# Graph kernel on one core: chunk offsets kept in bytes, both PSUM addresses of a chunk lowered together, one load of offsets moved from chunk 60 to chunk 47

## The chip, the cores and the metric

The kernel runs on one core of a Trainium2 chip. The metric is the device time of one execution in microseconds (us). PE is TensorE's matmul side, PEld its weight load, DVE VectorE, ACT ScalarE, POOL GpSimd, SP SyncE. "PEldq" in the rows is TensorE's sequencer: the part that reads the instruction stream, executes register instructions itself and passes weight loads and matmuls on to the array's queue.

## The reference, cut to what matters

Inputs are `x` (1024 nodes x 512 features, fp32), 16384 edges `src`, `dst` (sorted by `dst`) with weights, and six weight matrices of 512x512 with their biases.

```python
A[src, dst] += edge_weight;  A = dinv * A * dinv          # dinv from the row sums of A
h = x
for l in 0, 1:
    h = leaky_relu(((A @ h) @ W_gcn[l] + b_gcn[l]) @ W_mlp[l] + b_mlp[l])
x = layernorm(x + h)
h = gcn_conv(relu(gcn_conv(x, W1, b1)), W2, b2)           # edge counts plus self loops, both sides scaled by deg^-1/2
out = layernorm(x + h)
```

## The kernel before, in words

**The chunk loop** builds the dense adjacency. The 16384 edges are cut into 128 chunks of 128 edges. For a chunk DVE makes a one-hot matrix of the sources (`sel`) and four matrices over a window of 12 destinations (`hot`: plain counts and the edge weight in three bf16 parts). PE then runs four matmuls with `sel` as the stationary operand, each adding into 8 strips of 12 columns in PSUM: the count into one bank, the three weight parts into another (`chunk(c)`, L696 to L703). Where in the bank the window begins depends on the data: it is `offsets[c]`, a register value. `window(c, kind)` (L672) turns it into an address, with `kind` 0 for the weights and 1 for the counts, one bank of 512 fp32 further on.

**The offsets.** DVE computes them at the head of the kernel, in elements, and copies them from PSUM to the row `off_row` as int32 (L976). `load_offsets(c0)` (L666 to L670) loads 16 of them into 16 of the 32 registers and makes a value of each (`snap`). The eight calls stand in PE's stream: one ahead of the loop, and after chunks 15, 31, 47, 60, 73, 86 and 105 (the table `loads`, L248; L784). The registers are two halves of 16 that are used in turn, so the load for chunks 64 to 79 may stand anywhere after chunk 47. After chunk 60 there is also a `value_load` of a flag (L788), which says whether the data fit the windows.

**Work between the chunks.** The destinations form 20 overlapping regions, each accumulated in a pair of banks. At `opening[r]` PE clears the pair (`clear`, L676, after ACT has evacuated region r-2); after `closing[r]` ACT copies it to SBUF, and DVE adds the overlapping ends. The table `fillers` (L236) puts fp32 work into PE's stream after named chunks: transposes of the weights, products of pairs of weight matrices (`split_product`, L648), biases (L748, L741). After chunk 47 stand 14 matmuls of 512 columns (6 at L648, 8 at L748), then the load for 48 to 63; after chunk 60 stand 8 transposes (L634), then the load for 64 to 79, then the flag. From chunk 35 on each chunk has a fifth matmul, for the degrees (L707).

**The other engines in the loop.** DVE's order is written by hand (L1085 to L1131): it makes the batches of `hot` and `sel` (L989 to L997), and between them the low halves of the weights (L1069, L1082). For batches 4 to 7 ACT makes a share of the last term of `hot` (L503), at named chunks. Semaphores `made`, `scaled`, `batch_used`, `region_done` and `evacuated` tie the three engines.

**After the loop** PE runs some 1,150 fp32 matmuls, transposes among them: A transposed times x, products with the weights, the layer norms' rows, the second graph network, to the end at 336.0 us.

Of the kernel before, what the change touches and what calls it, by code (L numbers as in the profile page):

```python
# [5 lines left out]
F32 = mybir.dt.float32  # L6
F32R = mybir.dt.float32r
BF16 = mybir.dt.bfloat16
I32 = mybir.dt.int32
ALU = mybir.AluOpType  # L10
ACT = mybir.ActivationFunctionType
AX = mybir.AxisListType

P = 128
BANK = 512
# [7 lines left out]
REGION = 52  # L23
# [7 lines left out]
def gnn_resnorm(nc, x, src, dst, weight, wg, bg, wm, bm, w1, b1, w2, b2, out):  # L31
# [35 lines left out]
    with ExitStack() as ctx:  # L67
# [108 lines left out]
        off_row = at("off_row", SM, [1, P], I32)  # L176
# [49 lines left out]
        max_row = small[0:1, 199:200]  # L226

        psum = ctx.enter_context(nc.psum_tensor("psum", [P, 8, BANK], F32))
        flat = psum.rearrange("p b n -> p (b n)")


        FILL, WIDE = (5, 6, 7), (4, 5, 6, 7)
# [12 lines left out]
        filling = [(name, i) for c in sorted(fillers) for name, i, k0, k1 in fillers[c] if k1 == KD]  # L245


        loads = {15: 16, 31: 32, 47: 48, 60: 64, 73: 80, 86: 96, 105: 112}  # L248
        ring += [("prep", 0, 5), ("prep", 1, 6), ("prep", 2, 7), ("prep", 3, 4), ("deg", 0, 4)]
        n_fill = [0]  # L250

# [20 lines left out]
        def bank(name, i=0):  # L272
            return psum[:, place[(name, i)], :]
# [31 lines left out]
        prep = sem("prep")  # L305
# [4 lines left out]
        off_ready, spill_ready, flag_ready = sem("off_ready"), sem("spill_ready"), sem("flag_ready")  # L310
# [300 lines left out]
        def _(pe):  # L611
# [52 lines left out]
            offsets = {}  # L664

            def load_offsets(c0):  # L666
                own = regs[c0 % (2 * G):c0 % (2 * G) + G]
                pe.load(own, off_row[0:1, c0:c0 + G])
                for j, r in enumerate(own):
                    offsets[c0 + j] = pe.snap(r, min_val=0, max_val=2 * BANK + REGION - 1)  # L670

            def window(c, kind):  # L672
                return flat[:, bass.ds(offsets[c] + kind * BANK, BANK)]\
                    .rearrange("p (h d) -> p h d", d=PITCH)[:, :, 0:WINDOW]

            def clear(r):  # L676
# [19 lines left out]
            def chunk(c):  # L696
                buf, own = where(c)
                stationary = sel[buf][:, own, :]
                for k in range(4):
                    moving = hot[buf][:, k, own, :].rearrange("p (h d) -> p h d", d=WINDOW)  # L700
                    ins = pe.matmul(window(c, 1 if k == 0 else 0), stationary, moving,  # L701
                                    start=False, stop=False, skip_group_check=True)
                return ins  # L703

# [54 lines left out]
            for c in range(CH):  # L759
                if c in batch_of:  # L760
                    pe.wait_ge(made, sets_made(batch_of[c]))
                    if batch_of[c] in SHARED:
                        pe.wait_ge(scaled, G * (1 + list(SHARED).index(batch_of[c])))
                for r in range(NR):
                    if opening[r] == c:
                        clear(r)
                ins = chunk(c)
                if c in closing:
                    ins.then_inc(region_done, 1)
                if c >= LATE_HW:  # L770
                    ins = degree(c)
                    if c + 1 in batch_of:
                        ins.then_inc(batch_used, 1)
                    if c == CH - 1:
                        ins.then_inc(loop_done, 1)
                if c == LATE_HW - 1:
                    pe.wait_ge(hw_made, 1)
                    for k in range(LATE_HW):
                        ins = degree(k)
                        if k + 1 in batch_of:  # L780
                            ins.then_inc(batch_used, 1)
                for name, i, k0, k1 in fillers.get(c, []):
                    filler(name, i, k0, k1)
                if c in loads:  # L784
                    load_offsets(loads[c])
                if c == closing[8]:
                    pe.wait_ge(flag_ready, 1)
                    uncovered = pe.value_load(flags[0:1, 0:1], min_val=0, max_val=1)  # L788


            with pe.If(uncovered > 0):
                pe.wait_ge(gen_ready, 1)
                for n, b in enumerate((dst_f, gen_src, w_e)):
                    ins = pe.transpose(psum[:, 0, n * P:(n + 1) * P], b[:], ident[:])
                ins.then_inc(gen_turned, 1)
                with pe.Fori(0, 2 * NB) as t:
                    with pe.Fori(0, CH) as c:
                        pe.wait_ge(gen_ready, t * CH + c + 2)
                        for kind in range(2):
                            ins = pe.matmul(psum[:, kind, :], gen_sel[:], gen_hot[:, kind, :], start=True, stop=True)  # L800
# [29 lines left out]
            for j in range(NB):  # L830
                pe.wait_ge(low_made["at"], j + 1)
                pe.wait_ge(x_low_made, j + 1)
                for f in range(KD):
                    s = slice(f * P, (f + 1) * P)
                    ins = split_product(bank("g1_a", f), [(x_high[:, j, s], x_low[:, j, s])], [at_parts(0, j)],
                                        first=(j == 0), end=(j == NB - 1))
# [18 lines left out]
            b = claim("deg1")  # L855
            for n in range(NB):
                ins = pe.matmul(b[:, n:n + 1], cnt_sums[:, n * P:(n + 1) * P], ones_col, start=True, stop=True)  # L857
# [78 lines left out]
        def _(dve):  # L936
# [7 lines left out]
            def after(count):  # L944
# [8 lines left out]
            b = then(dve.tensor_scalar(hi_i[:], src_i[:], 7, None, ALU.arith_shift_right))  # L953
            dve.wait_ge(dst_in, 16)
            c = then(dve.tensor_copy(dst_f[:], dst_i[:]))
# [8 lines left out]
            b = then(dve.scalar_tensor_tensor(out=jumped, in0=bounds, scalar=base, in1=jumps,  # L964
                                              op0=ALU.is_le, op1=ALU.mult))
# [7 lines left out]
            dve.scalar_tensor_tensor(out=col_f[:], in0=hi_f[:], scalar=float(WINDOW), in1=rel_f[:],  # L973
                                     op0=ALU.mult, op1=ALU.add).then_inc(edge_ready, 1)
            dve.wait_ge(prep_done, 3)
            dve.tensor_copy(off_row[:], bank("prep", 2)[0:1, 0:P]).then_inc(off_ready, 1)  # L976

            def make(n, k):
                b, count = BATCHES[n]
# [382 lines left out]
```

## Time and profile before

| | us |
|---|---|
| median of 3 runs | 339.26 (338.84 to 339.58) |
| the profiled execution | 337.82 |
| its span (first to last instruction) | 336.0 |
| outside the span, 337.82 - 336.0 | 1.82 |

The page gives the mean granted TensorE clock as 0.996 of full speed. In a row of the timeline the first number is the start in us from the span's start, the second the length; `x4` means that four instructions are merged. Matmuls overlap (each lasts longer than the distance to the next one), so the rate is read from starts, not from lengths.

### The profile page before, as it was taken

The numbers are of one execution on the slowest core, as the hardware profiler recorded it, in microseconds if no ns is written. First come the engines' busy times: TensorE is split into PE (matmuls) and PEld (weight loads), VectorE is DVE, ScalarE is ACT, GpSimd is POOL, SyncE is SP. The second block draws the span as 40 slices with busy tenths as digits, with TensorE's granted clock in tenths as the row PEclk, the third lists the DMA queues.
The fourth block names the chain that finished last, engine by engine and source line by source line (L and its number), as shares of the span: only waits on it lengthen the run. The fifth ranks groups of instructions, "written<-read, shape, count | busy, mean of one in ns | idle before, by whom it ended". The sixth has DMA issues, their size and how long they took to land.

```text
span 336.0 us, 5049 instructions
## 1 busy us (share of the span) xinstructions
PE 316.9 (94%) x1976; PEld 261.2 (78%) x1977; DVE 189.2 (56%) x333; ACT 122.0 (36%) x253; POOL 49.8 (15%) x54
## 2 busy tenths in 40 slices
PE   2988979999899999999999999999999999999993
PEld 1766776887688888888888888888888888888882
DVE  6998999623635431156642457675952344225664
ACT  3647886635543401033342013133702444220000
POOL 2100000001003990100000011212580000000111
PEclk9999999999999999999999999999999999999998
DMA  6270000610000000000510000005200000000121
GB/s 203 73 251 2 3 2 0 209 47 2 1 0 3 0 2 0 0 0 2 180 69 2 0 0 2 0 2 198 89 0 0 2 0 0 2 4 31 62 83 75
DMA packets 8591, 13.45 MB, mean 40 GB/s; under 512 B 1906, under 2 KB 2290, under 8 KB 8564
## 3 DMA queue, kind: packets, MB, share of 16 engines
q1 hardware_dynamic: 8564, 13.05, 11.3%
q8 instruction: 21, 0.34, 0.4%
q14 instruction: 6, 0.05, 0.0%
HBM read 10.95 MB, written 2.10 MB: 39 GB/s over the span
## 4 chain that ended last, share of the span: by engine, by line
PE 88%; DVE 7%; issue 2%; ACT 1%; DMA 1%; POOLq 0%; POOL 0%; SPq 0%; ACTq 0%
PE psum L648 74%; PE psum L701 6%; PE psum L634 3%; DVE hot L997 2%; PE psum L748 1%; DVE sel L989 1%; PE psum L823 1%; DVE hot L992 1%; PE psum L689 1%; DVE wgt_low L1069 1%; DVE wm_low L1082 1%; DMA src_i<-in_src 1%; PE psum L707 1%; PE psum L857 1%; ACT hot L453 0%
## 5 line engine op out<-in xcount | busy, mean ns | idle before, releaser
L701 PE MATMUL psum<-hot,sel 128*128 128x96 bf16 x512 | 34.8, 215 | 3.1 <-issue 2.1
L701 PEld LDWEIGHTS psum<-hot,sel 128*128 128x128 bf16 x512 | 29.9, 101 | 9.7 <-issue 8.2
L439 POOL TENSOR_TENSOR small<-small 128x1 f32<-128x1 f32 x16 | 11.9, 742 | 161.8 <-DVE small L1265 161.8
L648 PE MATMUL psum<-at_high,x_high 128*128 128x512 f32 x64 | 25.8, 403 | 0.6 <-DVE x_low L1193 0.6
L1069 DVE SCALAR_TENSOR_TENSOR y_low<-psum,small,y_high 128x512 fp32r<-128x512 f32 x16 | 11.9, 750 | 24.2 <-ACT y_high L453 24.2
L648 PE MATMUL psum<-at_low,x_high 128*128 128x512 f32 x64 | 25.1, 391 | 0.0
L648 PE MATMUL psum<-y_high,at_high 128*128 128x512 f32 x64 | 25.0, 391 | 0.0
L648 PE MATMUL psum<-at_high,x_low 128*128 128x512 f32 x64 | 24.9, 390 | 0.0
L648 PE MATMUL psum<-y_low,at_high 128*128 128x512 f32 x64 | 24.9, 389 | 0.0
L648 PE MATMUL psum<-y_high,at_low 128*128 128x512 f32 x64 | 24.9, 389 | 0.0
L648 PE MATMUL psum<-cnt,x_high 128*128 128x512 f32 x64 | 24.9, 389 | 0.0
L648 PE MATMUL psum<-cnt,x_low 128*128 128x512 f32 x64 | 24.9, 389 | 0.0
L648 PE MATMUL psum<-y_high,cnt 128*128 128x512 f32 x64 | 24.9, 389 | 0.0
L648 PE MATMUL psum<-y_low,cnt 128*128 128x512 f32 x64 | 24.9, 389 | 0.0
L1069 DVE SCALAR_TENSOR_TENSOR g_low<-psum,g_high 128x512 fp32r<-128x512 f32 x16 | 10.2, 683 | 25.9 <-ACT g_high L453 25.9
L453 ACT ACTIVATE g_high<-psum 128x512 fp32r<-128x512 f32 x16 | 8.6, 608 | 33.2 <-PE psum L648 33.2
L584 ACT ACTIVATE xs<-tmp,small 128x512 f32<-128x512 f32 x8 | 6.5, 816 | 38.3 <-DVE small L1277 38.3
L453 ACT ACTIVATE y_high<-psum,small 128x512 fp32r<-128x512 f32 x16 | 10.9, 688 | 25.1 <-PE psum L648 25.0
L997 DVE TENSOR_TENSOR hot<-hot,tables 128x1536 bf16<-128x1536 bf16 (+2 forms) x27 | 19.7, 776 | 0.3
L1228 DVE TENSOR_TENSOR tmp<-psum,col_scale 128x512 f32<-128x512 f32 x16 | 11.0, 689 | 14.8 <-PE psum L648 14.8
L1069 DVE SCALAR_TENSOR_TENSOR at_low<-psum,at_high 128x512 fp32r<-128x512 f32 x16 | 10.7, 687 | 15.3 <-ACT at_high L453 15.3
L453 ACT ACTIVATE adj<-psum 128x512 f32<-128x512 f32 (+2 forms) x27 | 12.4, 460 | 18.0 <-PE psum L701 18.0
(185 smaller groups left out, 755.1 us busy)
## 6 DMA issues: line engine op xcount, KB each, us to landing
wg_raw<-in_L_gnn_W_gcn SPq DMA_DIRECT2D x2, 1024.0 KB, 5.5
x_raw<-in_x SPq DMA_DIRECT2D x1, 2048.0 KB, 8.9
xs<-in_x SPq DMA_DIRECT2D x1, 2048.0 KB, 9.1
w_raw<-in_L_gnn_W SPq DMA_DIRECT2D x2, 1024.0 KB, 7.9
out<-xs SPq DMA_DIRECT2D x8, 256.0 KB, 2.0
wm_raw<-in_L_gnn_W_mlp SPq DMA_DIRECT2D x1, 1024.0 KB, 8.5
wm_next<-in_L_gnn_W_mlp SPq DMA_DIRECT2D x1, 1024.0 KB, 7.8
bias_bc<-in_L_gnn_b SPq DMA_DIRECT2D x1, 256.0 KB, 8.1
```

Of the source, the lines that this page charges most:

```text
L439: pool.tensor_tensor(r[:, 1:2], r[:, 0:1], power[:, 0:1], ALU.pow).then_inc(rstd_ready, 1)
L453: return act.activation(dest, source, ACT.Copy, **kw)
L584: act.activation(xs[:, i, :], tmp[:, i % 3, :], ACT.Identity, bias=shift[:, i % 2:i % 2 + 1], scale=rstd[:, 2 * (i % 2) + 1:2 * (i % 2) + ...
L634: ins = pe.transpose(dest[:, n * P:(n + 1) * P], b, ident[:])
L648: ins = pe.matmul(dest, s, m, start=first and n == 0, stop=end and n == len(pairs) - 1, skip_group_check=True)
L689: pe.matmul(ends, none[:], zeros[:, 0:2 * COLS].rearrange("p (h a d) -> p h a d", h=NB, a=2), start=True, stop=False, skip_group_check=True)
L701: ins = pe.matmul(window(c, 1 if k == 0 else 0), stationary, moving, start=False, stop=False, skip_group_check=True)
L707: return pe.matmul(bank("deg")[:, 0:3 * NB].rearrange("p (a h) -> p a h", a=3), sel[buf][:, own, :], hw[:, :, c, :], start=(c == 0), stop= ...
L748: ins = pe.matmul(b[0:2, :], bg_parts[:, k, :], m[:, k, :], start=(k == 0 and n == 0), stop=(k == KD - 1 and n == 1))
L997: ins = dve.tensor_tensor(sums(k - 1), sums(0), column(k + 1, COLS), ALU.mult)
L1069: dve.scalar_tensor_tensor(out=dest, in0=tile, scalar=scale, in1=high.bitcast(F32), op0=ALU.mult, op1=ALU.subtract).then_inc(low_made[name ...
L1228: dve.tensor_tensor(tmp[:, r % 3, :], bank(name, n), col_scale[:, h * BANK:(h + 1) * BANK], ALU.mult).then_inc(taken[name], 1)
```

## The change

`off_row` now holds 4 times the offset, that is bytes. The view of PSUM is one of bytes (`uint8`), sliced at the byte offset and seen as fp32 again. `chunk(c)` makes its two windows first and calls `lower_ap` on both before the first matmul, where before each matmul's window was lowered on its own. The bounds given to `snap` are in bytes, with the statement that the value is a multiple of 4. The table `loads` holds lists, and the load for chunks 64 to 79 stands after chunk 47, behind the one for 48 to 63.

```diff
-        flat = psum.rearrange("p b n -> p (b n)")
+        flat_bytes = psum.rearrange("p b n -> p (b n)").bitcast(U8)
...
-        loads = {15: 16, 31: 32, 47: 48, 60: 64, 73: 80, 86: 96, 105: 112}
+        loads = {15: [16], 31: [32], 47: [48, 64], 73: [80], 86: [96], 105: [112]}
...
-                    offsets[c0 + j] = pe.snap(r, min_val=0, max_val=2 * BANK + REGION - 1)
+                    offsets[c0 + j] = pe.snap(r, min_val=0, max_val=4 * (2 * BANK + REGION - 1),
+                                              guaranteed_mod_val=0, out_of_modulus=4)
...
-                return flat[:, bass.ds(offsets[c] + kind * BANK, BANK)]\
+                return flat_bytes[:, bass.ds(offsets[c] + 4 * kind * BANK, 4 * BANK)].bitcast(F32)\
                     .rearrange("p (h d) -> p h d", d=PITCH)[:, :, 0:WINDOW]
...
                 stationary = sel[buf][:, own, :]
+                sums = [window(c, kind) for kind in range(2)]
+
+                for w in sums:
+                    pe.lower_ap(w)
                 for k in range(4):
                     moving = hot[buf][:, k, own, :].rearrange("p (h d) -> p h d", d=WINDOW)
-                    ins = pe.matmul(window(c, 1 if k == 0 else 0), stationary, moving,
+                    ins = pe.matmul(sums[1 if k == 0 else 0], stationary, moving,
                                     start=False, stop=False, skip_group_check=True)
...
-                if c in loads:
-                    load_offsets(loads[c])
+                for c0 in loads.get(c, []):
+                    load_offsets(c0)
...
-            dve.tensor_copy(off_row[:], bank("prep", 2)[0:1, 0:P]).then_inc(off_ready, 1)
+            dve.tensor_scalar(off_row[:], bank("prep", 2)[0:1, 0:P], 4.0, None, ALU.mult).then_inc(off_ready, 1)
```

## Rows read from the trace of the kernel before

**Rows 1.** Stretches: start:end, length, then each engine's busy us and instructions, clock, DMA.
```profile
0.00:26.67 26.67, 17.22 (x168) 13.20 (x168) 23.19 (x55) 13.07 (x32) 2.77 (x18) 1.00 0.50 166
26.67:48.66 21.99, 21.99 (x261) 18.09 (x261) 20.59 (x34) 17.95 (x52) 0.77 (x2) 1.00 0.01 2
48.66:50.55 1.89, 0.01 (x2) 0.01 (x1) 1.86 (x3) 1.10 (x3) 0.00 (x0) 1.00 0.04 9
50.55:81.00 30.45, 29.52 (x401) 23.79 (x403) 16.34 (x24) 17.53 (x51) 0.00 (x0) 1.00 0.21 70
```
**Rows 2.** Chain that ended last, in order of time: start, length, what.
```profile
23.84 1.11 ACT hot L453 x4
...
48.66 1.88 issue
...
79.29 0.38 PE psum L683
```
**Rows 3.** Line L668 (registers' load), whole span, and 47.9:50.4 with L670 and L788.
```profile
L668 PEldq TENSOR_LOAD <-off_row x8: 1102/1108/1309, 6.4 to 71.5; - x8
...
L668 PEldq TENSOR_LOAD <-off_row x1: 1105/1105/1105, 48.0 to 48.0; - x1
...
L670 PEldq FUSED_REGOPS  x2: 125/152/180, 49.2 to 49.6; - x2
...
L788 PEldq TENSOR_LOAD <-flags x1: 305/305/305, 49.8 to 49.8; - x1
```
**Rows 4.** Timeline of PE before and after that load.
```profile
47.52 1.14 PE L634 MATMUL psum<-ident,wg_raw 128*128 128x128 f32 x8
50.55 0.42 PE L701 MATMUL psum<-hot,sel 128*128 128x96 bf16 x4 [1.88 <-issue]
```
**Rows 5.** L668 and L670 in 38:42, behind chunk 47; PE's timeline there.
```profile
L668 PEldq TENSOR_LOAD <-off_row x1: 1102/1102/1102, 38.9 to 38.9; - x1
...
L670 PEldq FUSED_REGOPS  x2: 125/152/180, 40.1 to 40.3; - x2
...
39.03 0.49 PE L648 MATMUL psum<-wm_high,wgt_high 128*128 128x512 f32 x1
...
42.38 0.35 PE L701 MATMUL psum<-hot,sel 128*128 128x96 bf16 x4
```
**Rows 6.** Line L701 on the sequencer in 50.4:50.9.
```profile
L701 PEldq FUSED_REGOPS  x4: 42/46/51, 50.4 to 50.8; - x4
```
**Rows 7.** PE's timeline: chunks 51, 52 and 53, their first four matmuls.
```profile
43.20 0.33 PE L701 MATMUL psum<-hot,sel 128*128 128x96 bf16 x4
...
43.39 0.36 PE L701 MATMUL psum<-hot,sel 128*128 128x96 bf16 x4
...
43.61 0.33 PE L701 MATMUL psum<-hot,sel 128*128 128x96 bf16 x4
```
**Rows 8.** PE's timeline: chunks 62, 106 and 127, and what follows 127.
```profile
50.83 0.40 PE L701 MATMUL psum<-hot,sel 128*128 128x96 bf16 x4
...
73.19 0.42 PE L701 MATMUL psum<-hot,sel 128*128 128x96 bf16 x4 [0.23 <-issue]
...
80.51 0.42 PE L701 MATMUL psum<-hot,sel 128*128 128x96 bf16 x4
...
80.80 0.48 PE L648 MATMUL psum<-wm_high,wgt_high 128*128 128x512 f32 x1
```
**Rows 9.** Timeline of DVE, ACT and PE: what PE's stream waits for; chunk 80.
```profile
47.26 1.29 DVE L1069 SCALAR_TENSOR_TENSOR wgt_low<-psum,wgt_high 128x512 fp32r<-128x512 f32 x2
...
58.23 2.21 ACT L453 ACTIVATE hot<-hot,last_term 128x96 bf16<-128x96 bf16 x8
...
61.20 0.37 PE L701 MATMUL psum<-hot,sel 128*128 128x96 bf16 x4
```
**Rows 10.** DVE's timeline: the copy that becomes a product, and a product of like size.
```profile
5.50 0.28 DVE L976 CAST off_row<-psum 1x128 int32<-1x128 f32 x1 [0.25 <-PE psum L659]
...
35.89 0.21 DVE L1030 TENSOR_SCALAR step_row<-step_row 1x127 f32<-1x127 f32 x1
```

More of the change, by code:

```diff
@@ L9 @@
 I32 = mybir.dt.int32
+U8 = mybir.dt.uint8
 ALU = mybir.AluOpType
```

## The prediction

> **What bounds the kernel now.** I cut the span into stretches first and then asked the chain of waits, line by line, what ends each idle stretch of PE. In the first 26.67 us PE is busy 17.22 us and DVE 23.19: DVE makes the one-hot batches and PE waits [rows 1]. I cut at 26.67 because the chain runs over DVE and ACT until there (ACT's share of batch 4, at 23.84, is one of its last pieces [rows 2]) and over PE from there on. From then on PE is the bound. From 26.67 to 48.66 it is busy without a hole; then come 1.89 us in which it does nothing, although DVE works on; from 50.55 to 81.00 it is busy 29.52 of 30.45 us [rows 1]. The chain has the hole as 1.88 us of "issue": PE's array waited for no other engine, but for its own sequencer [rows 2].
>
> The sequencer's own rows say what it did. At 48.0 it began the load of 16 registers of line L668, which took 1,105 ns, then two fused register instructions of `snap` (L670; 125 to 180 ns), and at 49.8 the flag's load (L788, 305 ns) [rows 3]. Ahead of it stood the 8 small transposes that began at 47.52, so PE had 0.66 us of work left when the load started (47.52 + 1.14 - 48.0); the next chunk began at 50.55 [rows 4]. Each of the eight loads takes 1.10 to 1.31 us [rows 3]; most are hidden, since long fillers stand ahead of them. Behind chunk 47 the load starts at 38.9, before the first of 14 fp32 matmuls (39.03), and chunk 48 begins at 42.38 [rows 5].
>
> Second cost: addresses. Before, a chunk costs two register instructions of 42 to 51 ns. Four of them start between 50.4 and 50.8, so they follow each other at about 0.12 us, and a chunk costs the sequencer 0.24 to 0.25 us [rows 6]. PE itself needs 0.19 to 0.22 us for a chunk with its degree matmul: chunks 51 to 53 start at 43.20, 43.39 and 43.61, when matmuls had queued up behind a filler [rows 7]. So the sequencer falls behind in runs of chunks and catches up during fillers. Where it has no lead, behind the load of chunk 60 for instance, a chunk takes 0.28 (50.55 to 50.83) [rows 4, 8].
>
> **The change, step by step.**
>
> Load of 64 to 79 away from chunk 60. From its start at 48.0 to the flag's load at 49.8 lies one load with its two snaps: 1.8 us by the two rounded starts, 1.41 by the three durations with the gaps between them left out [rows 3]. I take 1.75. The flag's load and its wait stay. They then start at 48.0, last as long as now, and chunk 61 starts at 48.80 in place of 50.55; the transposes end at 48.66, so 0.14 us of the hole remain. Gain **1.75**.
>
> The same load behind chunk 47. It issues one TENSOR_LOAD and two snaps on PE's sequencer, no DMA, and passes no queue of SP or POOL. The first load with its snaps ends at 40.4 (starts 38.9, 40.1 and 40.3, the last one 0.125 long [rows 5]). The second takes 1.5 us (as this one) to 1.75 (as the one of chunk 60), so it ends between 41.9 and 42.2. From the first register instruction of a chunk to its first matmul passes some 0.15 us (50.4 to 50.55 [rows 4, 6]): chunk 48 could start at 42.1 to 42.4, and starts at 42.38 now [rows 5]. The cover is 3.35 us of fp32 work and is just used up. Without it the second load would cost its full 1.75. With the semaphores between, I take **+0.05** (bounds 0 and +0.25). What PE gains or loses up to chunk 60 counts little in any case: the last four transposes there wait for DVE's `wgt_low` that begins at 47.26 and ends, the first of the two, at about 47.9 [rows 9], in a stretch in which DVE is busy 20.59 of 21.99 us [rows 1]. So gains before 48 are lost, and for the same reason nothing ahead of 26.67 counts.
>
> One address instruction in place of two, after 48. The sequencer then needs some 0.13 us a chunk (one interval of rows 6), less than the array's 0.21, and the array's own time decides everywhere. What comes back is the excess of the chunks that run without a lead. There are 13: 61 and 62; 87 and 88 (behind the load of chunk 86); 106 to 108 and 111 (behind the one of chunk 105, whose first chunk starts at 73.19); 115 to 118; and 127, at 80.51, with the next matmul at 80.80 [rows 8]. Their periods, the clears taken off, sum to 3.53 us, from 0.28 for the first to 0.29 for the last; at 0.21 they would take 2.73. Gain **0.80**. If the joint instruction costs as much as two (0.25 us), the gain is 0. Chunks 119 to 121 don't count: clear(19), at 79.29 [rows 2], waits for ACT to evacuate region 17, and that follows chunk 118 at a fixed distance.
>
> The 0.23 us of idle before 73.19 [rows 8] stays, since that load can't start earlier. When the load behind chunk 47 starts, at 38.9, 14 fp32 matmuls and the last 3 of that chunk are still to run [rows 5]: 17 queued, and counted in the same way the sequencer is never further ahead in the loop; behind chunk 105 (71.5, the last of the eight [rows 3]) it has 16. The Trainium skill says otherwise: "TensorE: Matmul & The Clock Gate", on engine queue depths, gives TensorE 64 entries. With a lead of that size a faster sequencer would hide this load too and the sum would be 0.23 larger; 17 weight loads with 17 matmuls are 34 entries, and a lead limited there is what the trace bears out.
>
> DVE's product in place of a copy (L976, 0.28 us) is on the head's chain; a product of like size takes 0.21 [rows 10]. Between -0.07 and +0.07, I take 0.
>
> Who is late next, with PE 1.9 us earlier? ACT's second share of batch 7 starts at 58.23 and ends at 60.44, chunk 80 begins at 61.20 [rows 9]; ACT's chain there starts from PE's bias product behind chunk 66, so both move together and about 0.7 us of slack stay. Of the 30.45 us after the hole DVE is busy 16.34 [rows 1]. No row shows another engine taking over.
>
> Sum: 1.75 - 0.05 + 0.80 = **2.5 us**. The profiled execution (337.82, of which the span is 336.0) would be 335.3. The median is 1.44 above that execution, so for it 339.26 - 2.5 = **336.8**.
>
> **The rivals.**
>
> Only the move works: the addresses are still made in two instructions or the joint one is twice as long. For it: the rows show fused instructions of up to 180 ns [rows 3]. Against it: two additions are less than what one fused instruction does now (a product and a sum). 339.26 - 1.7 = 337.6.
>
> The second load isn't covered, or DVE/ACT hold PE up after 48: a new wait of 1 to 1.5 us in place of the one removed, 338.1 to 338.6. For it: the cover behind chunk 47 is used to within 0.2 us, and PE is next to DVE's pace before 48. Against: durations of L668 hardly vary. The Trainium skill has a rule that makes this dearer: "Runtime: NRT & Kernel Launch", on instruction fetch mechanics, gives about 200 ns a register for such loads, which for 16 registers would be 3.2 us and for two loads 3 us more than the cover; the trace's 1.1 us for 16 (69 ns each) disagrees. By that rule the time would be some 339.8; I give it 0.01, inside the 0.03 of the last rival but one.
>
> Slower: the joint instruction becomes the bound. Its place is every chunk, its price is bounded by the snap's instruction, 0.18 us long with up to 0.22 us behind it: 0.40 us a chunk against 0.21. Between fillers lie 6 or 7 chunks, of which 3 are queued ahead; a stretch would lose 6.5 x 0.19 - 0.6 = 0.64 us, ten stretches 6.4, the move gives 1.7 back: 344.0. It decides from about 0.33 us a chunk. Against it: the present two instructions show 0.12 each.
>
> Nothing comes: the program does the same in another place, 339.3.
>
> More than forecast: the sequencer, faster now, gets further ahead of the array than the 17 matmuls counted, and the 0.23 us before chunk 106 goes too [rows 8]: 336.5.
>
> **How the numbers follow.** The forecast 0.73; only the move 0.09; a new wait 0.08; nothing 0.03; slower 0.04; and 0.03 for more than forecast. The range for 8 in 10 starts below the forecast by the remaining idle and the scatter of a median (335.9) and reaches past "only the move" into the new wait (338.3). No change means within 0.2%, 0.68 us, about what a measurement of this kernel can tell: faster is 0.73 + 0.09 + 0.03 + half of the new wait, 0.89; same 0.07; slower 0.04.
>
> **What would show it.** Right: no TENSOR_LOAD at L668 near 48, two in a row from 38.9; "issue" before chunk 61 falls from 1.88 to about 0.15; 127 or 128 register instructions at L701 in place of 256; chunks 61, 87, 106 and 116 with periods of 0.20 to 0.22; chunk 48 within 0.2 us of 42.4. Wrong: a hole before chunk 48, a wait for `scaled` or `made` before chunk 80 or 96, or register instructions more than 0.2 us apart.

## The result, and the profile after

| us | before | after |
|---|---|---|
| median beside each other | 338.84 (337.18 to 339.58, 5 executions) | 335.11 (334.92 to 335.88, 5 executions) |
| the profiled execution | 337.82 | 335.47 |
| its span | 336.0 | 333.6 |

The ratio is 0.9905, with a 95% interval of 0.9877 to 0.9933. The kernel is faster, as forecast, and by more: 335.11 lies 1.7 us below the forecast (336.8) and 0.8 us below the low end of its range. The two executions of before that were added here, 337.65 and 337.18, already lie 1.2 and 1.7 us below the lowest of the three that the forecast had (338.84 to 339.58). That is the thread which leads to the error.

First the head of the page of the changed kernel, and the group of the chunks' matmuls (busy us, mean ns of one, then the idle time before them and who ended it).

```profile
span 333.6 us, 4919 instructions
...
PE 314.5 (94%) x1977; PEld 259.7 (78%) x1977; DVE 189.0 (57%) x333; ACT 122.0 (37%) x253; POOL 49.9 (15%) x54
...
L708 PE MATMUL psum<-hot,sel 128*128 128x96 bf16 x512 | 32.3, 215 | 2.1 <-DVE hot L1004 1.3
```

Then the stretches of [rows 1], cut at the same events: end of the head, start and end of the hole behind chunk 60, start of the last clear.

```profile
0.00:26.46 26.46, 15.52 (x167) 12.33 (x168) 23.18 (x55) 13.06 (x32) 2.85 (x18) 1.00 0.53 167
26.46:48.35 21.89, 21.89 (x261) 18.00 (x261) 20.50 (x34) 18.01 (x53) 0.78 (x2) 1.00 0.01 2
48.35:48.49 0.14, 0.00 (x1) 0.01 (x1) 0.14 (x1) 0.14 (x2) 0.00 (x0) 1.00 0.00 0
48.49:78.53 30.04, 28.76 (x402) 23.08 (x403) 17.96 (x26) 18.28 (x52) 0.00 (x0) 1.00 0.21 72
```

The hole of 1.89 us is 0.14 us now. The chain of waits has it as "issue" again, between the transposes and chunk 61. Of the other entries of that kind in the loop the one at 66.75 is new, and the one before chunk 106, at 71.08, is the old one:

```profile
47.30 1.05 PE psum L636 x8
48.35 0.14 issue
48.49 0.34 PE psum L708 x4
...
66.75 0.39 issue
...
71.08 0.24 issue
```

What was the sequencer doing? Its rows by line: the address instructions of all chunks and of a stretch late in the loop, the two loads behind chunk 47 with their `snap`s, and the flag's load, now directly behind the transposes. Three of the 128 records of L705 are missing from the trace.

```profile
L705 PEldq FUSED_REGOPS  x125: 37/37/42, 8.0 to 77.6; - x125
...
L670 PEldq TENSOR_LOAD <-off_row x2: 1102/1102/1103, 38.6 to 40.2; - x2
...
L672 PEldq FUSED_REGOPS  x4: 125/152/180, 39.7 to 41.6; - x4
...
L795 PEldq TENSOR_LOAD <-flags x1: 310/310/310, 47.7 to 47.7; - x1
```

And PE's timeline: the first matmul behind chunk 47, chunk 48, the transposes, chunks 61 and 62, chunks 87 and 88 (behind the load of chunk 86), the stall in chunk 99, and chunks 106 and 107.

```profile
38.72 0.49 PE L650 MATMUL psum<-wm_high,wgt_high 128*128 128x512 f32 x1
...
42.06 0.35 PE L708 MATMUL psum<-hot,sel 128*128 128x96 bf16 x4
...
47.15 1.20 PE L636 MATMUL psum<-ident,wg_raw 128*128 128x128 f32 x8
48.49 0.34 PE L708 MATMUL psum<-hot,sel 128*128 128x96 bf16 x4
...
48.70 0.36 PE L708 MATMUL psum<-hot,sel 128*128 128x96 bf16 x4
...
62.13 0.34 PE L708 MATMUL psum<-hot,sel 128*128 128x96 bf16 x4
...
62.34 0.33 PE L708 MATMUL psum<-hot,sel 128*128 128x96 bf16 x4
...
66.44 0.31 PE L708 MATMUL psum<-hot,sel 128*128 128x96 bf16 x3
...
67.14 0.22 PE L708 MATMUL psum<-hot,sel 128*128 128x96 bf16 x1 [0.39 <-issue]
...
71.32 0.34 PE L708 MATMUL psum<-hot,sel 128*128 128x96 bf16 x4 [0.24 <-issue]
...
71.53 0.36 PE L708 MATMUL psum<-hot,sel 128*128 128x96 bf16 x4
```

To compare executions whose heads differ by tenths of a microsecond I count chunk starts from the start of chunk 31, and look at periods (start of a chunk to start of the next):

```
                       before    after    after again (e9)
chunk 48 starts at     15.532    15.423   15.417
60 -> 61                3.288     1.562    1.555
61 -> 62                0.284     0.207    0.207
87 -> 88                0.283     0.209    0.208
99 -> 100               1.704     2.246    1.693
105 -> 106              1.360     1.372    1.214
106 -> 107              0.283     0.207    0.207
chunk 127 starts at    53.666    51.544   50.824
```

The profiled execution of after gained 2.12 us up to chunk 127, and another 0.20 in the head, where the DMA of `src` took 1.93 us instead of 2.13. It lost 0.55 in chunk 99, and e9, which is the same program, did not: there the gain is 2.84: the 0.55 more, and another 0.16 behind chunk 105.

### The profile page after: what moved, and what is told of

Read it like the earlier page. It is cut to its first block, busy times and chain, and to the rows that moved or that the text cites. A ratio compares the mean times of both kernels' runs of the same rounds, so it can differ in the third digit from the quotient of the medians.

```text
span 333.6 us, 4919 instructions
## 1 busy us (share of the span) xinstructions
PE 314.5 (94%) x1977; PEld 259.7 (78%) x1977; DVE 189.0 (57%) x333; ACT 122.0 (37%) x253; POOL 49.9 (15%) x54
## 4 chain that ended last, share of the span: by engine, by line
PE 88%; DVE 7%; issue 2%; ACT 1%; DMA 1%; POOLq 0%; POOL 0%; SPq 0%; ACTq 0%
PE psum L650 75%; PE psum L708 6%; PE psum L636 3%; DVE hot L1004 2%; PE psum L755 1%; DVE sel L996 1%; PE psum L830 1%; DVE hot L999 1%; PE psum L692 1%; DVE wm_low L1089 1%; DVE wgt_low L1076 1%; PE psum L714 1%; DMA src_i<-in_src 1%; PE psum L864 1%; ACT hot L455 0%
## 5 line engine op out<-in xcount | busy, mean ns | idle before, releaser
L708 PE MATMUL psum<-hot,sel 128*128 128x96 bf16 x512 | 32.3, 215 | 2.1 <-DVE hot L1004 1.3
L708 PEld LDWEIGHTS psum<-hot,sel 128*128 128x128 bf16 x512 | 28.4, 101 | 7.5 <-issue 6.9
```

Source lines behind the costliest of these rows:

```text
L708: ins = pe.matmul(sums[1 if k == 0 else 0], stationary, moving, start=False, stop=False, skip_group_check=True)
```

## The experiments

The kernels ran on three chips (e1 to e4; e5 to e8; e9 to e12), each group with its own executions of the kernel before. "Clock" is an execution's mean granted clock.

**e1: the kernel before once more.** No edit.

> The kernel before, unchanged, once more beside itself. Its six executions so far lie between 337.2 and 339.6 us, the changed kernel's between 334.9 and 335.9; the forecast took the difference of the profiled execution to the median (1.44 us) as a constant of both kernels. Theory A (the spread is from execution to execution or from chip to chip, and belongs to both kernels): the ratio to itself is 1.000 within 0.3%, its executions spread over 1 us or more again. Theory B (the kernel before has a costlier variant of its run that the profiled execution did not catch, such as a longer stall around an instruction fetch): executions fall in two groups near 337.4 and 339.2, and a profile of one in the upper group shows a hole on PE that the profile shown does not have.

Measured: 337.88 us, median of 12; the executions of the kernel before beside it had a median of 339.01 (21); ratio 0.9983 (0.9964 to 1.0002). One program, two medians 1.1 us apart: the times are not one cloud. Sorted by clock they fall into two groups, with no clock between 0.992 and 0.995:

```
clock          e1, median (n)    before beside e1 to e4, median (n)
0.995 or more  337.83 (9)        337.69 (8)
0.990 to 0.992 338.96 (3)        339.20 (13)
```

Over all three chips, the executions of before beside the experiments are 45 at 0.995 or more (median 337.75) and 29 at 0.990 to 0.992 (median 339.16). By chip the shares are 8 to 13, 19 to 10 and 18 to 6. Two of the 45 have times like the lower group's all the same (339.47 and 339.20, both at 0.995), so the clock sorts nearly all of them, not every one. From here on every kernel is read at the upper clock first, and the number of its executions at the lower one is told beside it.

**e2, e3, e4: one part alone.** e2 has only the move, e3 only the addresses, e4 lowers the two windows together but keeps the offsets in elements.

```diff
 e2, against before
-        loads = {15: 16, 31: 32, 47: 48, 60: 64, 73: 80, 86: 96, 105: 112}
+        loads = {15: [16], 31: [32], 47: [48, 64], 73: [80], 86: [96], 105: [112]}
 e3, against after
-        loads = {15: [16], 31: [32], 47: [48, 64], 73: [80], 86: [96], 105: [112]}
+        loads = {15: [16], 31: [32], 47: [48], 60: [64], 73: [80], 86: [96], 105: [112]}
 e4, against before
+                sums = [window(c, kind) for kind in range(2)]
+                for w in sums:
+                    pe.lower_ap(w)
...
-                    ins = pe.matmul(window(c, 1 if k == 0 else 0), stationary, moving,
+                    ins = pe.matmul(sums[1 if k == 0 else 0], stationary, moving,
```

> Only the load for chunks 64 to 79 is moved from chunk 60 to chunk 47; addresses as before. Theory 1 (the two edits add up, the load's part is what the forecast says): 1.7 us less than the kernel before (ratio 0.995), chunk 48 delayed by 0 to 0.25 us, the hole before chunk 61 down from 1.88 to 0.15 us. Theory 2 (the moved load is worth more than its hole, since the median fell by 3.2 to 3.7 us): 2.5 us or more.

> Only the addresses: offsets in bytes, both lowered ahead of the first matmul, the load for 64 to 79 still behind chunk 60. Theory 1: 0.8 us less than the kernel before in the profile (ratio 0.9975), chunks 61, 62, 87, 88, 106 to 108, 111 and 115 to 118 at 0.20 to 0.22 us each. Theory 2 (127 instructions less mean fewer or other instruction fetches, so more than the chunks' excess is won): 1.5 us or more, and the difference sits outside the chunks named.

> Both windows are lowered together ahead of the first matmul, but the offsets stay in elements and off_row is copied as before; the load stays behind chunk 60. Theory 1 (what counts is that the sequencer has one instruction instead of two, not how much it computes): one register instruction a chunk, 5 to 15 ns longer than in bytes, time equal to the addresses-only kernel within 0.1 us in the profile. Theory 2 (bytes are what makes it cheap, since the product by 4 must be made twice): register instruction of 80 ns or more, chunks without a lead at 0.24 us or more, and less than half of the 0.8 us.

Measured, all against 339.01:

```
     median (n)    ratio (95%)                 upper clock (n)  lower (n)   60 -> 61
e2   336.03 (6)    0.9918 (0.9894 to 0.9942)   336.02 (6)       - (0)       1.509
e3   336.74 (6)    0.9935 (0.9911 to 0.9959)   336.75 (6)       - (0)       3.137
e4   336.78 (10)   0.9952 (0.9931 to 0.9974)   336.73 (7)       338.19 (3)  3.163
```

At the upper clock, against 337.75, the move is worth 1.73 us and the addresses 1.00. That makes 2.73; both together are worth 2.75 (e9, below). So the two parts add up, within what medians of six can tell, and the chunks show them in their places. In e2 chunk 61 follows the transposes after a short gap, but chunk 62 comes 0.28 us behind it, as in [rows 4, 8]:

```profile
47.51 1.14 PE L634 MATMUL psum<-ident,wg_raw 128*128 128x128 f32 x8
48.79 0.42 PE L701 MATMUL psum<-hot,sel 128*128 128x96 bf16 x4
...
49.07 0.41 PE L701 MATMUL psum<-hot,sel 128*128 128x96 bf16 x4
```

e4 does as well as e3 without bytes. Its address instruction is longer, but it is still one a chunk:

```profile
L702 PEldq FUSED_REGOPS  x128: 56/64/74, 8.4 to 79.1; - x128
```

**e12: bytes alone.** Offsets in bytes (the bounds given to `snap` too) and a byte view, but a window is lowered at each matmul, as before.

```diff
-        flat = psum.rearrange("p b n -> p (b n)")
+        flat_bytes = psum.rearrange("p b n -> p (b n)").bitcast(U8)
...
-                return flat[:, bass.ds(offsets[c] + kind * BANK, BANK)]\
+                return flat_bytes[:, bass.ds(offsets[c] + 4 * kind * BANK, 4 * BANK)].bitcast(F32)\
...
-            dve.tensor_copy(off_row[:], bank("prep", 2)[0:1, 0:P]).then_inc(off_ready, 1)
+            dve.tensor_scalar(off_row[:], bank("prep", 2)[0:1, 0:P], 4.0, None, ALU.mult).then_inc(off_ready, 1)
```

> Offsets in bytes, but each window still lowered at its own matmul: two register instructions a chunk, each computing less. Joint lowering with offsets in elements (one instruction of 64 ns) was as fast as with bytes (one of 37). Theory 1 (the sequencer's cost is per instruction): chunks without a lead take 0.24 us or more as in the kernel before, time equal to it within 0.2 us in each clock group. Theory 2 (what counts is what is computed): a third or more of the 0.8 us comes back.

Measured: 338.44 (12), ratio 0.9999 (0.998 to 1.0018). By the medians alone one would say that it does nothing. By clock, 4 executions at the upper have 336.91, so 0.84 us less than before, and 8 are at the lower with 338.54, 0.62 less than before's lower group. That is the expectation's Theory 2: most of the gain comes back without the number of instructions going down. There are still two register instructions for each chunk, but plain ones of 32 ns:

```profile
L703 PEldq ALU_OP  x253: 32/32/42, 8.3 to 81.3; - x127
```

Distances between the starts of address instructions where the sequencer has no lead, worked out from the traces:

```
                        instructions a chunk   length, ns   distances, us   a chunk
before                  2 fused                37 to 51     0.115, 0.129    0.244
e12, bytes alone        2 ALU_OP               32           0.112, 0.113    0.225
e4, joint in elements   1 fused                64           0.142           0.142
after                   1 fused                37           0.115           0.115
```

The distance is the instruction's own length plus 0.078 to 0.081 us each time, so most of what an address instruction costs doesn't depend on what it computes. But what the kernel gains doesn't follow the number of instructions alone: it follows the sum for a chunk against the array's 0.19 to 0.22. At 0.244 the sequencer falls behind quickly. At 0.225 it hardly does: in e12's trace the chunks next to a load still take 0.27 (61 and 106), but 87, 111 and 115, which take 0.26 to 0.30 in the kernel before, run at the array's pace (0.208, 0.221, 0.198). One instruction a chunk, of either form, is below the array's time everywhere and gives the whole gain.

**e5, e6, e7: what the hole costs.** e5 was meant to double the hole: the load behind chunk 60 stands there twice (`60: [64, 64]`). e6 and e7 are the kernel before unchanged, for profiles of other executions.

> The kernel before, with the load for chunks 64 to 79 issued twice behind chunk 60 (same registers, same values), so that PE's hole there is 3.6 us in place of 1.9. Executions of the kernel before fall in two groups, near 337.7 (mean granted clock 0.995 to 1.000) and near 339.2 us (0.990 to 0.992); the kernel with the load moved away has only the upper clock. Theory H (the hole itself now and then brings the clock down for a stretch right behind it): with the longer hole every execution has it, the profile shows the clock at its lower level right behind the hole and 96-column matmuls at about 80 ns in place of 42, and the time is 1.75 (load) + about 1.4 us above the lower group of before: 340.8 with nothing of two groups left. Theory E (the clock falls early at the end of the kernel, for a reason that has nothing to do with the hole): 339.5 and 340.9 in the same mixture as before, and a profile with the clock at its upper level through the loop.

> The kernel before once more, for a profile of an execution of its upper group. Theory H: if the execution is near 339.2, the lower clock stands behind 50.5 us in the profile and chunks 61 and on take more than 0.3 us. Theory E: the lower clock stands in the last 10 us alone.

> The same as the one before it: another draw of the kernel before. Theory H: an execution near 339.2 has the lower clock behind 50.5 us, one near 337.7 has not. Theory E: both have the upper clock through the loop and differ in the last 10 us.

e5 could not answer. Its trace still has eight loads and a hole of 1.71 us: the second, identical load did not run (where it was dropped, no row shows), so it is one more sample of the kernel before: 338.85 (10), ratio 1.0012 (0.9996 to 1.0029). e6 has 338.19 (8; 1.0001), e7 has 337.91 (8; 0.9991; one execution of 1121.96 is left out of what follows). e1, e5, e6 and e7 together have 22 executions at the upper clock and 15 at the lower.

The profiled executions of e6 and e7 were both in the lower group (339.19 and 339.42 us, clock 0.991), and they show where the time goes. e6 in stretches, from the end of the transposes: hole, chunks 61 and 62, the next 3.40 us, and what follows.

```profile
48.66:50.60 1.94, 0.30 (x3) 0.06 (x1) 1.91 (x4) 1.47 (x4) 0.00 (x0) 1.00 0.00 0
50.60:51.30 0.70, 0.69 (x11) 0.58 (x12) 0.70 (x2) 0.00 (x0) 0.00 (x0) 0.95 0.00 0
51.30:54.70 3.40, 3.40 (x29) 2.22 (x27) 3.40 (x7) 1.21 (x4) 0.00 (x0) 0.51 0.00 0
54.70:58.00 3.30, 3.30 (x44) 2.22 (x42) 3.27 (x5) 2.17 (x8) 0.00 (x0) 1.00 0.00 0
```

The granted clock (the third number from the end) is 1.00 before the hole, 0.51 in the 3.40 us behind chunk 62, that is 1.2 GHz, and 1.00 again after. PE is busy all the time there, but runs 29 matmuls where the profiled execution of before runs 46:

```profile
51.30:54.70 3.40, 3.40 (x46) 2.13 (x44) 3.40 (x6) 1.73 (x6) 0.00 (x0) 1.00 0.00 0
```

Chunk by chunk, in e6's timeline, 64 and 65 are 0.40 us apart there, and 67 and 68 are 0.21 apart again, at the full clock:

```profile
50.61 0.50 PE L701 MATMUL psum<-hot,sel 128*128 128x96 bf16 x4 [1.65 <-issue]
...
51.93 0.54 PE L701 MATMUL psum<-hot,sel 128*128 128x96 bf16 x4
...
52.33 0.54 PE L701 MATMUL psum<-hot,sel 128*128 128x96 bf16 x4
...
55.64 0.34 PE L701 MATMUL psum<-hot,sel 128*128 128x96 bf16 x4
...
55.85 0.36 PE L701 MATMUL psum<-hot,sel 128*128 128x96 bf16 x4
```

From chunk 61 to 67 the kernel before takes 3.44 us in its profiled execution, 5.03 in e6 and 4.94 in e7, so the lower clock costs 1.6 and 1.5 us. The groups' medians differ by 1.41.

Why the clock falls in one execution and not in the next, the traces let one see in part. The record of the clock begins when it first rises, in the head (the 1.00 of the stretches ahead of that rests on no record). The matmuls tell the rest: within the chunks around that moment they start 82 to 93 ns apart before it and 43 to 49 behind it. The same 24 matmuls of chunks 5 to 10 took 1.33 us in the profiled execution of before, 1.82 in e6 and 2.08 in e7:

```profile
12.46 1.33 PE L701 MATMUL psum<-hot,sel 128*128 128x96 bf16 x24
...
12.57 1.82 PE L701 MATMUL psum<-hot,sel 128*128 128x96 bf16 x24
...
12.44 2.08 PE L701 MATMUL psum<-hot,sel 128*128 128x96 bf16 x24
```

The clock rose at 13.7 us in e6 and at 14.1 in e7 and e12, the three profiles whose clock fell behind a hole of 1.65 to 1.89 us, and at 11.0 to 12.5 in the five with such a hole and no fall (before, e1, e3, e4, e5). In e8, where the hole is closed, it rose at 14.4 and didn't fall. From the rise to the fall passed 37.55 us in e6, e7 and e12, and in e10 (below) too. So where there is a hole, the moment of the fall goes with the moment of the rise and not with the end of the hole, and whether it comes at all goes with it too. These are nine profiles with a hole, and no run set the moment on purpose.

**e9: the changed kernel once more.** No edit.

> The changed kernel unchanged, beside the kernel before on one chip. In its profile a hole of 0.6 us stood inside chunk 99, with no wait that the profile shows, and its five executions lie between 334.9 and 335.9 us. Theory H (the lower clock behind chunk 60 comes from the hole that is gone): no execution with a granted clock under 0.994, and the difference to the executions of before with the upper clock is 2.5 us, to those with the lower clock 3.9. Theory F (the hole at chunk 99 is a late instruction fetch and a matter of the single execution): executions in 334.7 to 335.9, a profile with or without that hole.

Measured: 335.00 (334.61 to 335.24, 6 executions) beside 337.82 (24) of before; ratio 0.9911 (0.9889 to 0.9932). All six, and the five behind the result, are at the upper clock. In the profile the stall in chunk 99 isn't there; the fp32 matmuls follow the chunk at once:

```profile
66.72 0.36 PE L708 MATMUL psum<-hot,sel 128*128 128x96 bf16 x4
...
66.94 0.48 PE L650 MATMUL psum<-wm_high,wgt_high 128*128 128x512 f32 x1
```

**e10 and e11: a longer hole without the load of 16 registers, and a shorter one with it.** If the hole brings the clock down, it should do so whatever makes it. e10 is the changed kernel with an early wait for batch 7, so PE stands still for DVE; e11 is the kernel before with the flag's load away from the hole (it stands behind chunk 92).

```diff
 e10, against after, behind chunk 60
+                    pe.wait_ge(made, sets_made(7))
                     pe.wait_ge(flag_ready, 1)
 e11, against before
-                if c == closing[8]:
+                if c == 92:
```

> The changed kernel with one more wait ahead of the flag's load behind chunk 60: for DVE's batch 7, which is made at about 51.3 us. No load is added, PE only stands still for 2.8 us. Theory H (standing still brings the clock down, whatever the reason for it): most or all executions with a granted clock of 0.990 to 0.992, time 335.1 + 2.9 + 1.4 = 339.4 in those and 338.0 in the rest. Theory L (the register load or its instructions have to do with the clock): all executions at 338.0 with the upper clock.

> The kernel before, with the flag's load (and nothing else) behind chunk 92. The hole behind chunk 60 shrinks from 1.9 to about 1.2 us, the load for 64 to 79 stays. Theory H: the profile gives 0.65 us against the kernel before's 337.8, so 337.2; executions with the lower clock are rarer or gone, because the hole is shorter than in addresses-only (1.6 us, none in 6): the median falls by more than 0.65 where half of before's executions have the lower clock. Theory L (a load behind chunk 60 is enough): still a third to a half of the executions with the lower clock.

e10: 339.84 (7), ratio 1.0058 (1.0031 to 1.0084); all seven at a lower clock: five at 0.990 to 0.992, two at 0.986 and 0.987 with over 341 us, and the profile is of one of these two. Its stretches (the hole; behind it; then):

```profile
48.30:51.40 3.10, 0.00 (x0) 0.00 (x0) 3.07 (x4) 1.01 (x3) 0.00 (x0) 0.80 0.00 0
51.40:57.20 5.80, 5.50 (x40) 3.40 (x40) 5.46 (x8) 1.21 (x4) 0.00 (x0) 0.52 0.01 3
57.20:60.00 2.80, 2.80 (x41) 1.97 (x39) 0.95 (x2) 2.44 (x9) 0.00 (x0) 1.00 0.00 0
```

The clock falls while PE stands still (at 50.2 by the trace's record of it) and rises again at 57.0. In its timeline the cause of the hole is a wait and no register load, and the chunks behind it take 0.37 us instead of 0.21:

```profile
51.70 0.50 PE L708 MATMUL psum<-hot,sel 128*128 128x96 bf16 x4 [3.43 <-DVE hot L1005]
...
52.07 0.53 PE L708 MATMUL psum<-hot,sel 128*128 128x96 bf16 x4
```

e11: 336.82 (12), ratio 0.9958 (0.9943 to 0.9974), all twelve at the upper clock. The load of 16 registers stands where it stood, and the hole is 0.64 us shorter. (The median is 0.93 below before's upper group; where the other 0.3 us come from was not followed up.) Chunk 61 in its timeline:

```profile
49.87 0.42 PE L701 MATMUL psum<-hot,sel 128*128 128x96 bf16 x4 [1.24 <-issue]
```

Put together, with the shares that the kernel before has on the same chips:

```
hole behind chunk 60, us               lower clock   before, same chips
3.43  (e10)                            7 of 7        6 of 24
1.85  (e12)                            8 of 12       6 of 24
1.65 to 1.89 (before, e1, e5, e6, e7)  44 of 111
1.71 and 1.74 (e3, e4)                 3 of 16       16 of 33 (with e1)
1.24  (e11)                            0 of 12       6 of 24
0.14 and less (after, e9, e2, e8)      0 of 23
```

The ends of the table are clear: no execution has the lower clock where the hole is closed, and all have it behind 3.43 us, with no load of 16 registers in it. e11's 0 of 12 points the same way, though at the rate of 6 in 24 on its chip twelve without one would still come about by chance in 3 cases of 100. Between 1.65 and 1.89 us the length doesn't decide: e6 fell behind 1.65 and the profiled execution of before did not behind 1.88, and e12 has the lower clock more often than before, e3 and e4 less often, with holes of the same length. A hole of that length without a load in it was not tried.

**e8: a version that beats both.** The changed kernel with the last load moved on to chunk 99, and the flag's load behind chunk 92, under long fillers.

```diff
-        loads = {15: [16], 31: [32], 47: [48, 64], 73: [80], 86: [96], 105: [112]}
+        loads = {15: [16], 31: [32], 47: [48, 64], 73: [80], 86: [96], 99: [112]}
...
-                if c == closing[8]:
+                if c == 92:
```

> The changed kernel with its last two exposed loads behind longer fillers: the load for chunks 112 to 127 behind chunk 99 (6 fp32 matmuls) in place of chunk 105 (3), and the flag's load behind chunk 92 in place of chunk 60. Chunk 60 to 61 takes 1.56 us in the changed kernel against 1.2 of work, chunk 105 to 106 1.37 against 1.0. Theory 1 (both are exposed loads): both go, 0.6 to 0.7 us less than the changed kernel's 335.1, so 334.4, ratio to before 0.988. Theory 2 (the waits for DVE and ACT next to them take their place): less than 0.2 us.

Measured: 334.51 (334.40 to 334.76, 6 executions, all at the upper clock) beside 337.85 (29) of before; ratio 0.9888 (0.9867 to 0.9909), and about 0.5 us below the changed kernel (335.00 and 335.11, on other chips). Both remaining gaps are gone: chunk 61 follows the transposes 0.30 us sooner (60 -> 61 takes 1.260), chunk 106 follows its fillers at their own pace (105 -> 106 takes 0.977 where e9 has 1.214).

```profile
47.55 1.20 PE L636 MATMUL psum<-ident,wg_raw 128*128 128x128 f32 x8
48.59 0.33 PE L708 MATMUL psum<-hot,sel 128*128 128x96 bf16 x4
...
70.23 0.39 PE L650 MATMUL psum<-wm_low,wgt_high 128*128 128x512 f32 x1
70.46 0.34 PE L708 MATMUL psum<-hot,sel 128*128 128x96 bf16 x4
```

## Why the prediction was right and wrong

**The step that failed** is "The median is 1.44 above that execution, so for it 339.26 - 2.5 = 336.8". It carried the distance between the median and the profiled execution over to the changed kernel, as if it belonged to the measurement. It belonged to the old kernel. By their times the three executions of before came from its lower-clock group (338.64 to 339.61 in the 29 seen later; the clocks of these three are not on record), the profiled one (337.82, clock 0.996) from its upper group, and the groups are apart because the clock falls behind the hole of chunk 60. The change closes that hole, so the changed kernel has no lower group: 0 of 11 executions. The sum made against the profiled execution, "337.82 ... would be 335.3", was the right forecast for it: the profiled execution came to 335.47, with a stall of 0.55 us in it, and the medians to 335.11 and 335.00. No rival had this, for the forecast counted the hole at its own length alone. It had even named the 1.44 without asking why three executions all lie above the fourth by that much.

**Load away from chunk 60**, 1.75: e2 shows 1.73 by the median, and 60 -> 61 shrinks by 1.78 in e2 and by 1.73 in e9. The 0.14 us of "issue" that the forecast left there is there.

**The second load behind chunk 47**, +0.05 (0 to 0.25): it cost nothing. The period of chunk 47 is 3.543 us in before, e2, e3 and e9 alike. The starts tell why: first matmul at 38.72, chunk 48 at 42.06, 3.34 us apart, as before (3.35 [rows 5]), with both loads and four `snap`s between.

**One address instruction in place of two**, 0.80: e3 gives 1.00. The 13 chunks came out as forecast: the periods of 61, 87, 106 and 116 went to 0.207, 0.208, 0.207 and 0.195, and the 13 together gained 0.82 in e9. Chunks 119 and 120 got shorter too, and as forecast this did not count, since the clear behind 121 waited longer (121 -> 122: 1.335 before, 1.464 in e9). Two things were undersized. "So gains before 48 are lost": chunks 33 and 34 gained 0.13 us, and most of it was still there at chunk 48 (15.532 before, 15.417 in e9: 0.12) and at chunk 60 (20.414 and 20.281: 0.13). And "the 0.23 us of idle before 73.19 stays": in e9 105 -> 106 takes 0.15 less. The load starts 0.42 us ahead of chunk 105 there instead of 0.37, with 17 matmuls queued instead of 16, and from the last `snap` behind it to chunk 106 pass 0.22 us instead of 0.32. In the profiled execution of after the idle time is 0.24 as before: from the load's start to its first `snap` pass 1.33 us there, and 1.17 in e9 and before.

From 2.5 to what e9's profile shows: up to chunk 127 it gained 2.84, and 2.94 with chunk 127's own 0.10, which the forecast counted. Of these 0.44 us the 0.13, the 0.15 and the 0.05 that the second load did not cost are 0.33, and the rest is in gains of 0.01 to 0.03 in other chunks (66, 86, 112). By medians at the upper clock it is 2.75.

**The sequencer's lead.** Counted at each load, the sequencer was again never ahead by more than 17 matmuls with their 17 weight loads. The Trainium skill's 64 entries ("TensorE: Matmul & The Clock Gate", engine queue depths) are not borne out by any trace here, with 17 and 17 as the most in each of the 14 profiles. Its 200 ns a register ("Runtime: NRT & Kernel Launch", instruction fetch mechanics) was the wrong figure to hold against this load: the page defines TENSOR_LOAD as a load of registers from HBM, and `off_row` lies in SBUF. Here two loads of 16 took 1.10 us each, 69 ns a register.

**DVE's product** in place of the copy was taken as 0. The head's length differs by 0.21 us between the two profiles, but the DMA of `src` at its start differs by 0.20, so nothing of it is shown to come from the product.

**The rivals.** Only the move: excluded by e3, in which the addresses alone are worth 1.00. A new wait: there is no hole before chunk 48, nor before 80 or 96. A joint instruction that bounds: its starts are 0.115 us apart, not 0.40. More than forecast: partly so, by 0.15 of the 0.23 us before chunk 106, about a third of it by one matmul more in the queue (17, never beyond) and the rest by less time behind the last `snap`.

**What stays open.** The stall in chunk 99 ("issue" of 0.39 at 66.75) takes 0.55 us in the profiles of after and e3 and 0.87 in e10's, and is missing in those of e9 and e8; after and e9 are one program, so it is a matter of single executions. The traces show one thing that goes with it. DMA packets of the instruction queue (q8) come every 6 to 12 us behind chunk 47 in the other eleven profiles (in e9 at 49.98, 59.54 and 66.90); in the three with the stall a gap of 15 us lies ahead of it (in after from 49.50 to 64.65, with chunk 99 at 66.44). That would fit a sequencer short of instructions; it is not shown that the late packet is the cause. What sets the moment at which the clock rises in the head was not looked for either. The shares of lower-clock executions of one program are 16 of 33, 22 of 54 and 6 of 24 on the three chips, and 13 of 21 and 3 of 12 on one and the same, so a difference between chips isn't clear of chance.

## What to carry to other kernels

Before a forecast is moved from a profiled execution to a median, read the granted clock of all executions: where the times fall into two groups, ask which stretch makes them, and whether the change touches it. A hole of PE in an otherwise busy stretch can cost more than its length, here 1.4 us on top of 1.9 in two executions of five. Register loads are cheap under long fillers and dear behind short ones, and address work on the sequencer is to be held, as a sum for each chunk, against the array's time for it: the number of instructions makes most of that sum, and 8% less (0.225 in place of 0.244 us) was worth most of the gain where the two were this close.

## What was not expected of the hardware

- TensorE's granted clock fell from 2.4 to 1.2 GHz behind a hole of 1.65 to 1.89 us (e6, e7, e12), between stretches in which it was busy without a break; by their mean clock this was so in 44 of 111 executions of one program; behind 1.24 us in none of 12, with 3.43 in 7 of 7. Back at 2.4 GHz it was 3.4 us after the fall in e6, and 6.8 in e10. The fall came 37.55 us after the clock's rise in the head in all four profiles that have one, up to 1.1 us behind the end of the hole, and in e10 inside it. Chunks took 0.37 to 0.40 us instead of 0.20 to 0.22 in between. The Trainium skill ("TensorE: Matmul & The Clock Gate", the HAM clock gate) says that the point of transition depends on where it falls in a window that doesn't start with the kernel. The nine profiles fit that, as above: the outcome goes with when the clock rose. No run here shows the window itself.
- An address instruction costs the sequencer about 0.08 us beyond its own execution: distances of 0.112 us for 32 ns, 0.115 for 37, 0.129 for 51, 0.142 for 64. (Behind a `snap` of 165 to 190 ns it is 0.06.) Two plain instructions therefore save little of the sequencer's time against two fused ones (0.225 against 0.244 us a chunk), and one fused instruction in their place saves half; the kernel gained 0.84 and 1.00 us by them.
- A register load written twice in a row ran once (e5: eight loads in the trace, not nine).
